# Transformer layer with a mixture of experts on one core: where the last softmax sums, the layer norms and the square roots stand in the expert stage

## The chip, the cores and the metric

One core of one Trainium2 chip runs the whole kernel. The metric is device time in microseconds (us) of one execution. TensorE is PE in the profile, with its weight loads as PEld; VectorE is DVE, ScalarE is ACT, GpSimd is POOL, and SyncE, which here only issues DMAs, is SP.

## The reference

The input is x of shape (2, 2048, 256): two batches of 2048 tokens. Cut to what matters:

```python
x = x + _layernorm(attn(_layernorm(x)))       # 16 heads of 64, relative position bias, softmax, output projection
x = x + _layernorm(ffn(_layernorm(x)))
# attn: softmax(q k^T + bias) v, all heads side by side, @ wo
# ffn, for E = 8 experts, K = 2:
pooled = x.mean(axis=1)
logits = pooled @ gate_w.T + gate_b
gates = softmax(where(logits < second largest, -inf, logits))
expert_out = gelu(einsum('bsd,eod->beso', x, expert_w) + expert_b)
return einsum('be,beso->bso', gates, expert_out)
```

There are four kinds of layer norm over the 256 features of a token: on x, on the attention's output, on the sum that goes into the experts, and on the experts' output. Each one needs mean and variance, a square root, a reciprocal and one scaled copy of the tile.

## The kernel before

Every engine has its own hand-written program, and semaphores join them. An engine works strictly in the order of its program: a wait holds back everything behind it.

**Attention** takes about 2740 us. It goes over 8 pairs of heads, for each over 8 slots (2 batches x 4 chunks of 512 queries) and 16 key tiles: TensorE makes scores, ScalarE takes exp into a ring `prob` of 8 buffers, GpSimd adds the probabilities of a slot into `acc` (15 additions, line 541), TensorE multiplies them with v into the bank `po`. At the end of a slot `denominators` sums `acc` over the partitions (line 642), ScalarE copies that to `den_s` (`sums_of_psum`), a DMA reshapes it, VectorE inverts it, ScalarE and GpSimd split the inverse in two halves, a DMA brings it back and `inverses` spreads it to all partitions; `normalise_output`, `high_output`, `low_output`, `output` and `add_output` follow. For the last slot (`G_ALL`) all of this happens at the start of the expert stage.

**The expert stage** is a loop over 128 units (b, t, m), which I also number n = 64 b + 16 t + m: batch b, chunk t of 512 tokens, and m = 0 to 15, two halves for each of the 8 experts. A unit is 6 matmuls of 512 columns on TensorE into one of 4 PSUM banks (`expert`, line 869), a gelu on ScalarE (line 1222) into one of 16 slots of the same ring `prob`, and on VectorE a multiply-add by the gate into `acc` (`expert_sum`, lines 1589 and 1594). TensorE can start unit n when the gelu of unit n-4 is done. After the fifth unit of the next chunk TensorE transposes a chunk's result into the two banks `pre` (`back`, line 834), and VectorE copies it to `y` (`ft_copy`, line 1599).

Everything else is written in between by hand, at fixed m, on each engine:

- layer norms: `tile_sums` and `variances` on VectorE (lines 1459, 1466 and 1468), `norm_sqrt` on ScalarE (line 1059, one table load for it and one back to gelu), `deviations` on VectorE (lines 1477 to 1487, six small instructions), and the scaled copies on ScalarE (line 1063), 4 tiles of 128 tokens at a time, in `norm_in_place` or, into the buffer `xn`, in `norm_tokens`; `add_rows` on VectorE (line 1496) adds the residual;
- for batch 1, in chunk (0,3), four groups of tokens are handed through two banks: `spare_transposes` on TensorE (line 846), `high_spare` on ScalarE (line 1085), `low_spare` on VectorE (line 1552). Group g+1 can only be transposed when `low_spare` of group g is done, since the banks `po` and `pm` are the same;
- the gate of a batch: `gate_log`, `gate_head`, `gate_rows`, `gate_tail`.

The norms' numbers are `LN_RES[1]` (attention's output, batch 1), `LN_FF[1]` (experts' input, batch 1), `LN_OUT` (experts' output, batch 0) and `LN_LAST` + chunk (experts' output, batch 1, a norm for each chunk). Behind the loop stand the last chunk's `back`, `ft_copy`, sums, norm, addition and the output DMA.

## Time and profile before

| what | us |
|---|---|
| median of 3 runs | 2971.9 (2971.86 to 2973.07) |
| the profiled execution, its own time | 2971.88 |
| its span, first to last instruction | 2970.1 |
| PE busy in the span | 2836.7 (96%) |
| first expert unit starts at | 2747.98 |
| last instruction of VectorE starts at, lasts | 2965.49, 1.23 |

Times in the trace are counted from the start of the span. An entry such as `[1.53 <-DVE ...]` behind an instruction says how long its engine had been idle before it, and what released it. The clock columns give the clock that TensorE was granted, 1.00 being 2.4 GHz.

### The profile page before, as it was taken

How to read it: one execution, taken by the hardware profiler on the slowest of the kernel's cores; microseconds unless marked ns; L12 is line 12 of the kernel's file. 1: busy time of each engine (PE TensorE's matmuls, PEld its weight loads, DVE VectorE, ACT ScalarE, POOL GpSimd, SP SyncE). 2: the span in 40 equal slices, each digit the busy share in tenths (PEclk: the TensorE clock that was granted, in tenths of full speed). 3: DMA queues.
4: the chain of work that ended last, by engine and by line, in shares of the span. 5: the costliest groups of instructions: out<-in, count | busy, mean ns of one | idle time of the engine just before them, and what ended most of it. 6: DMA issues, size and time to landing. Idle time of an engine off the chain costs nothing.

```text
span 2970.1 us, 49731 instructions
## 1 busy us (share of the span) xinstructions
PE 2836.7 (96%) x18785; PEld 1048.1 (35%) x18785; DVE 1836.8 (62%) x4663; ACT 1672.6 (56%) x2182; POOL 2275.2 (77%) x1033
## 2 busy tenths in 40 slices
PE   5999999999999999999999999999999999988997
PEld 2333333333333333333333333333333333322443
DVE  7556655665656665665655566655665566685666
ACT  4555565555555555555555555555555555556576
POOL 0788888888888888988888898888888888977000
PEclk9999999999999999999999999999999999999999
DMA  5000000000000000000000000000000000100001
GB/s 158 19 1 1 1 19 1 1 1 2 19 2 1 1 19 2 1 1 19 1 1 1 1 19 1 2 1 19 1 1 1 1 9 2 58 1 29 1 1 57
DMA packets 45137, 35.73 MB, mean 12 GB/s; under 512 B 21554, under 2 KB 43314, under 8 KB 44898
## 3 DMA queue, kind: packets, MB, share of 16 engines
q1 hardware_dynamic: 44898, 32.56, 3.8%
q8 instruction: 148, 2.42, 0.3%
q14 instruction: 91, 0.75, 0.1%
HBM read 27.60 MB, written 10.55 MB: 13 GB/s over the span
## 4 chain that ended last, share of the span: by engine, by line
PE 50%; DVE 23%; issue 20%; ACT 4%; POOL 3%; DMA 0%; SPq 0%; DVEq 0%; ACTq 0%; POOLq 0%
PE po L633 17%; PE st L603 15%; PE pre L615 5%; DVE mpart L1330 4%; PE pm L570 4%; DVE st L1347 3%; DVE pre L1327 3%; PE st L869 3%; POOL acc L541 3%; DVE pre L1322 2%; PE pm L576 2%; PE pm L663 2%; ACT prob L959 1%; PE pm L642 1%; DVE y L1381 1%
## 5 line engine op out<-in xcount | busy, mean ns | idle before, releaser
L541 POOL TENSOR_TENSOR acc<-acc,prob 128x1024 f32<-128x1024 f32 x896 | 2115.9, 2361 | 383.2 <-ACT prob L959 303.3
L959 ACT ACTIVATE prob<-st 128x1024 f32<-128x1024 f32 x1024 | 1016.5, 1021 | 914.8 <-DVE st L1347 814.3
L633 PE MATMUL po<-prob,v 128*64 128x512 f32 x4096 | 994.8, 606 | 0.0
L603 PE MATMUL st<-qk 64*128 64x512 f16 x6144 | 836.0, 378 | 18.0 <-ACT prob L959 16.1
L1322 DVE CUSTOM_DVE_ANT_0 pre<-pre,ew 128x512 f32<-128x512 f32 x448 | 300.8, 713 | 560.4 <-issue 560.3
L1327 DVE CUSTOM_DVE_ANT_0 pre<-pre,tab 128x512 f32<-128x512 f32 x704 | 475.2, 715 | 144.2 <-issue 144.2
L603 PEld LDWEIGHTS st<-qk 64*128 64x128 f16 x6144 | 293.6, 95 | 346.5 <-ACT prob L959 58.9
L633 PEld LDWEIGHTS po<-prob,v 128*64 128x64 f32 x4096 | 248.8, 136 | 440.8 <-issue 364.6
L603 PE MATMUL st<-eq,ek 64*128 64x512 f16 x2048 | 390.0, 377 | 0.0
L615 PE MATMUL pre<-qk 64*128 64x512 f16 x1600 | 309.5, 384 | 38.4 <-ACT ew L989 16.5
L1330 DVE TENSOR_REDUCE mpart<-pre 128x2 f32<-128x1024 f32 x224 | 274.0, 1223 | 97.9 <-PE pre L615 96.2
L1347 DVE TENSOR_TENSOR st<-st,t 128x512 f32<-128x512 f32 (+2 forms) x352 | 261.8, 744 | 6.9 <-PE st L603 6.9
L989 ACT ACTIVATE ew<-pre 128x1024 f32<-128x1024 f32 x224 | 227.1, 1014 | 67.2 <-PE pre L615 67.2
L615 PEld LDWEIGHTS pre<-qk 64*128 64x128 f16 x1600 | 77.4, 93 | 409.3 <-issue 141.4
L541 POOL TENSOR_TENSOR acc<-prob 128x1024 f32<-128x1024 f32 x64 | 150.7, 2355 | 84.7 <-ACT prob L959 84.7
L869 PE MATMUL st<-xh,ew 128*128 128x512 f16 x512 | 155.7, 386 | 17.8 <-ACT prob L1222 17.8
L1308 DVE SCALAR_TENSOR_TENSOR qk<-pm,qk 128x512 f16<-128x512 f32 x123 | 84.7, 689 | 134.8 <-ACT qk L940 134.8
L603 PEld LDWEIGHTS st<-eq,ek 64*128 64x128 f16 x2048 | 100.1, 94 | 122.4 <-issue 1.9
L1222 ACT ACTIVATE prob<-st,eb 128x512 f32<-128x512 f32 x128 | 84.0, 685 | 49.5 <-PE st L869 48.7
L663 PE MATMUL pm<-wo,o 128*128 128x256 f16 x774 | 108.2, 276 | 0.0
L1589 DVE SCALAR_TENSOR_TENSOR acc<-prob,gate,acc 128x512 f32<-128x512 f32 x112 | 80.7, 746 | 43.9 <-ACT prob L1222 43.3
L869 PE MATMUL st<-xl,ew 128*128 128x512 f16 x256 | 98.8, 386 | 0.0
(204 smaller groups left out, 2325.4 us busy)
## 6 DMA issues: line engine op xcount, KB each, us to landing
t_scratch<-w_scratch SPq DMA_DIRECT2D x2, 2688.0 KB
inv_r<-inv SPq DMA_DIRECT2D x260, 1.0 KB, 1.7
qk<-x SPq DMA_DIRECT2D x8, 512.0 KB, 5.6
out<-qk SPq DMA_DIRECT2D x8, 512.0 KB, 3.6
w<-w_pairs SPq DMA_DIRECT2D x8, 384.0 KB, 3.9
t2f<-t_scratch SPq DMA_DIRECT2D x8, 384.0 KB, 4.8
t<-t_scratch SPq DMA_DIRECT2D x8, 384.0 KB, 3.2
den_c<-den_s SPq DMA_DIRECT2D x130, 2.0 KB, 1.7
```

The lines of the kernel that those rows point to most:

```text
L541: nc.gpsimd.tensor_tensor(acc[g % 2][:, :, :], a, prob[:, n % RING, :, :], ALU.add).then_inc(sum_p, 1)
L603: last = nc.tensor.matmul(st[:, 2 * (n % 2) + h, :], w[64 * h:64 * h + 64, :], t[64 * h:64 * h + 64, :], start=(r == 0), stop=(r == len(te ...
L615: last = nc.tensor.matmul(pre[:, h, :], qh[b][64 * h:64 * h + 64, at:at + 128], keys[64 * h:64 * h + 64, :], start=True, stop=True)
L633: last = nc.tensor.matmul(po[64 * h:64 * h + 64, :], v[:, g // CHUNKS, j, 64 * h:64 * h + 64], prob[:, n % RING, h, :], start=(s == 0), st ...
L663: last = nc.tensor.matmul(bank[:, D * n:D * n + D], o, w, start=(r == 0), stop=(r == len(terms) - 1))
L869: last = nc.tensor.matmul(st[:, n % 4, :], w, a, start=(r == 0), stop=(r == len(terms) - 1))
L959: nc.scalar.activation(prob[:, n % RING, :, :], st[:, 2 * (n % 2):2 * (n % 2) + 2, :], ACT.Exp).then_inc(exp_done, 1)
L989: nc.scalar.activation(twin[:, :, :], pre[:, :, :], ACT.Relu).then_inc(pre_used, 2)
L1322: nc.vector.tensor_tensor_reduce(pre[:, h, :], pre[:, h, :], twin[:, h, :], 1.0, NEG, ALU.add, ALU.max, mpart[:, c, h, t, kc:kc + 1, 0]).t ...
L1327: nc.vector.tensor_tensor_reduce(pre[:, h, :], pre[:, h, :], tab[:, h, at:at + 4, :].rearrange("p n u -> p (n u)"), 1.0, NEG, ALU.add, ALU ...
L1330: nc.vector.reduce_max(mpart[:, c, :, t, kc, 0], pre[:, :, :], AX.X).then_inc(pre_used, 2)
L1347: nc.vector.tensor_tensor(o, o, t1[:, :, at:at + hi - lo], ALU.add).then_inc(band_in, 1)
```

## The change

All of it lies behind the pairs of heads; the attention loop is untouched.

1. The last slot's `denominators` go from before the first expert unit to behind the third; ScalarE's `sums_of_psum` goes to before the gelu of m = 3, and the wait for all of GpSimd's additions is replaced by one for each gelu, for the buffer it overwrites. The other steps of this slot move by one to three units. On VectorE `gate_tail(0)` now stands ahead of `invert`.
2. Norms on ScalarE are done as two tiles at one unit and two at the next, not four at every first, second or fourth: `norm_pair`, and a `half` for `norm_tokens`.
3. The square root of `LN_FF[1]` goes from (0,2,10) to (0,2,15), that of `LN_OUT` from (1,1,0) to (1,1,2). In chunk (0,3) the transposes go from m = 2, 6, 10, 14 to 4, 7, 10, 14, `high_spare` and `low_spare` from 4, 8, 12 to 6, 9, 12. `add_and_sum` starts one unit earlier.
4. The norm of a finished chunk of batch 1 goes from m = 14 of the chunk during which its square root is taken to m = 0 and 1 of the following one, and its addition from m = 15 to m = 2 there; the last but one is done behind the loop.
5. The last chunk is no longer copied to `y` first: sums and norm read the banks `pre`. It is added and sent out in two halves.

```diff
@@ tensor
-            pe.wait_ge(y_add, G_ALL * YJ + 1)
-            denominators(G_ALL, 0)
...
                         expert(b, t, m)
+                        if (b, t, m) == (0, 0, 2):
+                            pe.wait_ge(y_add, G_ALL * YJ + 1)
+                            denominators(G_ALL, 0)
...
-                        if (b, t, m) == (0, 0, 8):
+                        if (b, t, m) == (0, 0, 10):
                             pe.wait_ge(den_row, G_ALL + 1)
                             inverses(G_ALL)
-                        if (b, t, m) == (0, 0, 12):
+                        if (b, t, m) == (0, 0, 14):
...
-                        if b == 0 and t == CHUNKS - 1 and m % 4 == 2:
-                            if m == 2:
+                        if (b, t) == (0, CHUNKS - 1) and m in (4, 7, 10, 14):
+                            if m == 4:
                                 pe.wait_ge(y_add, (G_ALL + 1) * YJ + 1)
-                            spare_transposes(B + 1, m // 4)
+                            spare_transposes(B + 1, (4, 7, 10, 14).index(m))
@@ scalar
+            def norm_pair(k, b, first, u):
+                norm_in_place(k, b, first, (first + 2 * u, first + 2 * u + 1)).then_inc(yn_set, 1)
...
-            sums_of_psum(G_ALL)
             act.wait_ge(pv_done, PAIRS * STEPS + RING)
-            act.wait_ge(sum_p, (G_ALL + 1) * SUMS)
...
+                        if (b, t, m) == (0, 0, 3):
+                            sums_of_psum(G_ALL)
-                        if (b, t, m) in ((0, 1, 13), (0, 1, 14), (0, 1, 15), (0, 2, 0)):
-                            g = (m - 13) % 16
-                            norm_in_place(LN_RES[1], 1, 0, range(4 * g, 4 * g + 4)).then_inc(yn_set, 1)
-                        if (b, t, m) == (0, 2, 10):
+                        if b == 0 and 13 <= 16 * (t - 1) + m < 21:
+                            norm_pair(LN_RES[1], 1, 0, 16 * (t - 1) + m - 13)
+                        if (b, t, m) == (0, 2, 15):
                             norm_sqrt(LN_FF[1])
-                        if (b, t, m) in ((0, 2, 13), (0, 2, 15), (0, 3, 5), (0, 3, 9)):
-                            norm_tokens(B + 1, 1, {13: 0, 15: 1, 5: 2, 9: 3}[m])
-                        if (b, t, m) in ((0, 3, 4), (0, 3, 8), (0, 3, 12), (1, 0, 0)):
-                            high_spare(B + 1, {4: 0, 8: 1, 12: 2, 0: 3}[m])
-                        if (b, t, m) == (1, 1, 0):
+                        if (b, t) == (0, 3) and m in (1, 2, 3, 4, 6, 7, 10, 11):
+                            u = (1, 2, 3, 4, 6, 7, 10, 11).index(m)
+                            norm_tokens(B + 1, 1, u // 2, u % 2)
+                        if (b, t, m) in ((0, 3, 6), (0, 3, 9), (0, 3, 12), (1, 0, 0)):
+                            high_spare(B + 1, {6: 0, 9: 1, 12: 2, 0: 3}[m])
+                        if (b, t, m) == (1, 1, 2):
                             norm_sqrt(LN_OUT)
-                        if (b, t) == (1, 1) and m in (6, 8, 10, 12):
-                            g = (m - 6) // 2
-                            norm_in_place(LN_OUT, 0, 0, range(4 * g, 4 * g + 4)).then_inc(yn_set, 1)
...
+                        if (b, t) == (1, 1) and 6 <= m < 14:
+                            norm_pair(LN_OUT, 0, 0, m - 6)
+                        if b == 1 and t >= 1 and m == 11:
+                            norm_sqrt(LN_LAST + t - 1)
+                        if b == 1 and t >= 2 and m < 2:
+                            norm_pair(LN_LAST + t - 2, 1, 4 * (t - 2), m)
                         act.wait_ge(ff_ready, n + 1)
-                        if n >= GE:
+                        if n < GE:
+                            act.wait_ge(sum_p, (G_ALL + 1) * SUMS - (GE - 1 - n) // 2)
+                        else:
                             act.wait_ge(ff_acc, n - GE + 1)
@@ vector
-                        if (b, t) == (0, 2) and m in (0, 2, 4, 6):
-                            add_and_sum(1, m // 2)
+                        if b == 0 and 16 * t + m in (31, 33, 35, 37):
+                            add_and_sum(1, (16 * t + m - 31) // 2)
-                        if (b, t) == (0, 3) and m in (4, 8, 12):
-                            low_spare(B + 1, m // 4 - 1)
+                        if (b, t) == (0, 3) and m in (6, 9, 12):
+                            low_spare(B + 1, m // 3 - 2)
...
             c = CHUNKS - 1
-            ft_copy(B - 1, c)
-            chunk_sums(1, c)
+            dve.wait_ge(ft_ready, B * CHUNKS)
+            for t in range(4):
+                tile_sums(LN_LAST + c, t, pre[:, t // 2, D * (t % 2):D * (t % 2) + D])
             variances(LN_LAST + c)
+            add_rows(1, c - 1, 6 * GROUPS + 2 * c)
             deviations(LN_LAST + c)
```

On TensorE, where the attention ends and the expert stage begins, before the change (L633 multiplies probabilities with v, L642 makes the last sums, L854 the gate's product, L869 is an expert unit):

```order
L633 MATMUL po<-prob,v 64x512
L642 MATMUL pm<-acc,unit 64x512 [waits sum_p,y_add]
L642 MATMUL pm<-acc,unit 64x512
L854 MATMUL po<-gwT,pooled 1x8 [waits consts_in,gv,o_out]
L854 MATMUL po<-gwT,pooled 1x8
L869 MATMUL st<-xh,ew 128x512 [waits xh_a,exp_done,xl_v,ew_lo,ew_hi]
```

The same place after it, where the lines are L635, L644, L854 and L869, from the last values to the sums; the rows left out are matmuls of units 0 to 2:

```order
L635 MATMUL po<-prob,v 64x512
L854 MATMUL po<-gwT,pooled 1x8 [waits consts_in,gv,o_out]
L854 MATMUL po<-gwT,pooled 1x8
L869 MATMUL st<-xh,ew 128x512 [waits xh_a,exp_done,xl_v,ew_lo,ew_hi]
...
L644 MATMUL pm<-acc,unit 64x512 [waits sum_p,y_add]
L644 MATMUL pm<-acc,unit 64x512
```

The sums and their wait for GpSimd (`sum_p`) now stand behind three units.

On VectorE in chunk (0,3), before the change (L1589 is an expert sum, L1552 the low halves of a handed-over group, L1599 the copy of the chunk before, out of `pre`):

```order
L1589 SCALAR_TENSOR_TENSOR acc<-prob,gate,acc 128x512 [waits ff_acc,gelu_done] x3
L1552 TENSOR_TENSOR xl<-po,xh 128x512 [waits xh_a]
L1552 TENSOR_TENSOR xl<-pm,xh 128x512 [waits xh_a]
L1589 SCALAR_TENSOR_TENSOR acc<-prob,gate,acc 128x512 [waits ff_acc,gelu_done] x2
L1599 COPY y<-pre 128x1024 [waits ft_ready]
```

The same place after it (L1604, L1614 and L1567):

```order
L1609 TENSOR_SCALAR acc<-prob,gate 128x512 [waits ft_ready,gelu_done] x2
L1604 SCALAR_TENSOR_TENSOR acc<-prob,gate,acc 128x512 [waits ff_acc,gelu_done] x5
L1614 COPY y<-pre 128x1024 [waits ft_ready]
L1567 TENSOR_TENSOR xl<-po,xh 128x512 [waits xh_a]
L1567 TENSOR_TENSOR xl<-pm,xh 128x512 [waits xh_a]
```

The copy, which stood two sums behind the first group's low halves, now stands directly ahead of them, and both stand behind the sum of m = 6.

On TensorE in the same chunk, after the change, between the first and the second group's transposes (L846; L834 is `back`); the rows left out are matmuls of units:

```order
L846 MATMUL pm<-ident,v 128x128 x4
L869 MATMUL st<-xh,ew 128x512 [waits gelu_done]
...
L834 MATMUL pre<-ident,acc 128x128 [waits ft_out,ff_acc]
L834 MATMUL pre<-ident,acc 128x128 x7
L869 MATMUL st<-xh,ew 128x512 [waits gelu_done]
...
L869 MATMUL st<-xh,ew 128x512 [waits gelu_done]
...
L846 MATMUL po<-ident,v 128x128 [waits xl_v,xh_a,xn_ready]
```

Three units (m = 5, 6, 7) lie between the two, where before there were four (m = 3 to 6).

## Rows read from the trace of the kernel before

**Rows 1.** The page, part 1: busy us (share of the span) and instructions.

```profile
PE 2836.7 (96%) x18785; PEld 1048.1 (35%) x18785; DVE 1836.8 (62%) x4663; ACT 1672.6 (56%) x2182; POOL 2275.2 (77%) x1033
```

**Rows 2.** Waits of PE from 2742 on: total us, times, longest.

```profile
PE st L869 <- ACT prob L1222: 17.8, 10, 6.5
```

**Rows 3.** Timeline of PE, start of the expert stage: start us, us, instruction, idle before.

```profile
2745.89 1.98 PE L642 MATMUL pm<-acc,unit 128*64 128x512 f32 x4 [3.70 <-POOL acc L541]
...
2747.98 1.03 PE L869 MATMUL st<-xh,ew 128*128 128x512 f16 x2
...
2752.23 0.38 PE L869 MATMUL st<-xl,ew 128*128 128x512 f16 x1
...
2752.88 0.38 PE L869 MATMUL st<-xl,ew 128*128 128x512 f16 x1
```

**Rows 4.** Timeline of ACT, the attention's last copy.

```profile
2742.24 0.60 ACT L994 ACTIVATE o_raw<-po 128x512 f32<-128x512 f32 x1 [5.34 <-PE po L633]
```

**Rows 5.** Timeline of ACT, norm of batch 1's attention output, groups of four tiles.

```profile
2794.33 2.07 ACT L1063 ACTIVATE y<-y,tab 128x256 f32<-128x256 f32 x4 [1.53 <-DVE tab L1487]
2796.31 0.67 ACT L1222 ACTIVATE prob<-st,eb 128x512 f32<-128x512 f32 x1
...
2798.84 0.67 ACT L1222 ACTIVATE prob<-st,eb 128x512 f32<-128x512 f32 x1
```

**Rows 6.** Timeline of PE in that norm and behind the next square root.

```profile
2797.03 0.61 PE L869 MATMUL st<-xh,ew 128*128 128x512 f16 x2 [1.25 <-ACT prob L1222]
...
2825.13 1.03 PE L869 MATMUL st<-xh,ew 128*128 128x512 f16 x2 [6.48 <-ACT prob L1222]
```

**Rows 7.** Timeline of ACT, square root of the experts' input norm.

```profile
2822.86 0.21 ACT L1059 ACTIVATE tab<-tab 128x16 f32<-128x16 f32 x1 [7.36 <-DVE tab L1468]
```

**Rows 8.** Windows of core 0: busy us (x count) of PE, PEld, DVE, ACT, POOL; granted clock.

```profile
2674.40:2679.00 4.60, 4.60 (x33) 1.60 (x33) 4.04 (x9) 4.04 (x5) 2.84 (x2) 1.00 0.00 0
2734.30:2739.50 5.20, 5.19 (x23) 1.74 (x23) 3.21 (x3) 1.90 (x2) 5.02 (x2) 0.67 0.37 128
2745.90:2751.80 5.90, 5.90 (x18) 1.76 (x19) 1.38 (x10) 2.87 (x4) 0.00 (x0) 0.50 0.02 3
2825.10:2830.30 5.20, 5.17 (x13) 1.87 (x14) 3.11 (x9) 3.67 (x7) 0.00 (x0) 0.50 0.00 0
```

**Rows 9.** Timeline of PE, the waits ahead of the first two of those windows.

```profile
2674.08 0.39 PE L615 MATMUL pre<-qk 64*128 64x512 f16 x2 [1.97 <-DVE mpart L1327]
...
2734.31 1.09 PE L603 MATMUL st<-qk 64*128 64x512 f16 x6 [2.05 <-ACT prob L959]
```

**Rows 10.** Timeline of ACT, DVE and PE: a group's hand-over in chunk (0,3).

```profile
2837.11 0.59 ACT L1085 ACTIVATE xh<-po 128x512 f16<-128x512 f32 x1
...
2839.65 0.68 DVE L1552 TENSOR_TENSOR xl<-po,xh 128x512 f16<-128x512 f32 x1
...
2848.03 0.63 PE L846 MATMUL po<-ident,v 128*128 128x128 f32 x4 [0.70 <-DVE xl L1552]
```

**Rows 11.** Timeline of ACT in chunk (1,1): both square roots, waits on DVE.

```profile
2884.10 0.22 ACT L1059 ACTIVATE tab<-tab 128x16 f32<-128x16 f32 x1 [2.44 <-DVE tab L1468]
...
2898.30 0.68 ACT L1222 ACTIVATE prob<-st,eb 128x512 f32<-128x512 f32 x1
...
2901.80 0.69 ACT L1222 ACTIVATE prob<-st,eb 128x512 f32<-128x512 f32 x1
...
2908.06 2.07 ACT L1063 ACTIVATE y<-y,tab 128x256 f32<-128x256 f32 x4 [2.46 <-DVE tab L1487]
```

**Rows 12.** Timeline of PE and DVE, the end of the kernel.

```profile
2956.62 1.97 PE L834 MATMUL pre<-ident,acc 128*128 128x128 f32 x8 [4.48 <-DVE acc L1589]
...
2958.63 1.22 DVE L1599 COPY y<-pre 128x1024 f32<-128x1024 f32 x1 [0.93 <-PE pre L834]
2959.89 1.41 DVE L1459 BATCH_NORM_STATS2 tab<-y 128x6 f32<-128x256 f32 x4
...
2965.49 1.23 DVE L1496 TENSOR_TENSOR qk<-qk,y 128x1024 f32<-128x1024 f32 x1 [2.14 <-ACT y L1063]
```

More of the change, by code:

```diff
@@ L509, in _ @@
                 sp.dma_start(out[0, QC * n:QC * n + QC, :].rearrange("(t p) d -> p t d", p=128), xr[:, at:at + 4, :]).then_inc(out_done, 16)
-            for n in range(GROUPS):
-                at = xr_tile(1, 4 * n)
+            for n in range(GROUPS + 1):
+                first, tiles = (4 * n, 4) if n < GROUPS - 1 else (4 * (GROUPS - 1) + 2 * (n - GROUPS + 1), 2)
+                at = xr_tile(1, first)
                 sp.wait_ge(res, 4 * GROUPS + n + 1)
-                sp.dma_start(out[1, QC * n:QC * n + QC, :].rearrange("(t p) d -> p t d", p=128), xr[:, at:at + 4, :]).then_inc(out_done, 16)
-            sp.wait_ge(out_done, 16 * B * GROUPS)
+                sp.dma_start(out[1, 128 * first:128 * (first + tiles), :].rearrange("(t p) d -> p t d", p=128),
+                             xr[:, at:at + tiles, :]).then_inc(out_done, 16)
+            sp.wait_ge(out_done, 16 * (B * GROUPS + 1))
         @block.gpsimd
@@ L1071, in norm_in_place, with norm_tokens @@
                 return last
-            def norm_tokens(k, b, g):
+            def norm_pair(k, b, first, u):
+                norm_in_place(k, b, first, (first + 2 * u, first + 2 * u + 1)).then_inc(yn_set, 1)
+            def norm_tokens(k, b, g, half):
                 act.wait_ge(e_inv, LN_OPS * (LN_FF[b] - B + 1))
                 act.wait_ge(tr_ready, k * GROUPS + max(g - 1, 0))
-                for t in range(4):
+                for t in (2 * half, 2 * half + 1):
                     last = norm_tile(LN_FF[b], 4 * g + t, xn[b][:, g % 2, D * t:D * t + D], xr[:, xr_tile(b, 4 * g + t), :])
-                last.then_inc(xn_ready, 1)
+                if half:
+                    last.then_inc(xn_ready, 1)
             def high_spare(k, g):
@@ L1213, in _ @@
-                        if b == 1 and t >= 1:
-                            c = t - 1
-                            if m == 11:
-                                norm_sqrt(LN_LAST + c)
-                            if m == 14:
-                                norm_in_place(LN_LAST + c, 1, 4 * c, range(4 * c, 4 * c + 4)).then_inc(yn_set, 1)
+                        if (b, t) == (0, 3) and m in (1, 2, 3, 4, 6, 7, 10, 11):
+                            u = (1, 2, 3, 4, 6, 7, 10, 11).index(m)
+                            norm_tokens(B + 1, 1, u // 2, u % 2)
@@ L1224, in _ @@
             c = CHUNKS - 1
+            for u in range(2):
+                norm_pair(LN_LAST + c - 1, 1, 4 * (c - 1), u)
+            c = CHUNKS - 1
             norm_sqrt(LN_LAST + c)
-            norm_in_place(LN_LAST + c, 1, 4 * c, range(4 * c, 4 * c + 4)).then_inc(yn_set, 1)
+            act.wait_ge(e_inv, LN_OPS * (LN_LAST + c - B + 1))
+            for u in range(2):
+                for n in (2 * u, 2 * u + 1):
+                    last = norm_tile(LN_LAST + c, n, y[:, TT + 4 * c + n, :], pre[:, u, D * (n % 2):D * (n % 2) + D])
+                last.then_inc(yn_set, 1)
         @block.vector
@@ L1663, in _ @@
             gate_head(0)
+            gate_tail(0)
             invert(G_ALL)
-            gate_tail(0)
             dve.wait_ge(xr_in[1], 16 * GROUPS)
@@ L1715, in _ @@
                                 deviations(LN_LAST + t - 1)
-                            if m == 15:
-                                add_rows(1, t - 1, 4 * GROUPS + t)
+                            if m == 2 and t >= 2:
+                                add_rows(1, t - 2, 6 * GROUPS + 2 * (t - 1))
             c = CHUNKS - 1
-            ft_copy(B - 1, c)
-            chunk_sums(1, c)
+            dve.wait_ge(ft_ready, B * CHUNKS)
+            for t in range(4):
+                tile_sums(LN_LAST + c, t, pre[:, t // 2, D * (t % 2):D * (t % 2) + D])
             variances(LN_LAST + c)
+            add_rows(1, c - 1, 6 * GROUPS + 2 * c)
             deviations(LN_LAST + c)
-            add_rows(1, c, 4 * GROUPS + c + 1)
+            for u in range(2):
+                dve.wait_ge(yn_set, 6 * GROUPS + 2 * c + u + 1)
+                at, xat = TT + 4 * c + 2 * u, xr_tile(1, 4 * c + 2 * u)
+                to = xr[:, xat:xat + 2, :].rearrange("p t d -> p (t d)")
+                nc.vector.tensor_tensor(to, to, y[:, at:at + 2, :].rearrange("p t d -> p (t d)"), ALU.add).then_inc(res, 1)
 def kernel(L0_attn_hidden_states, L0_attn_wq, L0_attn_wk, L0_attn_wv, L0_attn_wo, L0_attn_rel_bias,
```

12 lines of the change are left out of this document (6 added, 6 removed).

## The prediction, on record before the changed kernel ran

> **What bounds the kernel now.** I began with the busy line of the page: TensorE is busy for 96% of the span, GpSimd for 77%, ScalarE for 56% [rows 1]. That is an average over an attention stage that the change leaves alone and an expert stage of 222 us (2748 to 2970) that it rearranges, so I looked only at the second. There the list of TensorE's waits [rows 2] names ScalarE: 17.8 us in 10 waits for a gelu that came late. Then I read the timelines at each wait. At full clock three matmuls of a unit start within 0.65 us (2752.23 to 2752.88) [rows 3], so a unit is 1.295 us and 128 units are 166 us. From the first unit to the end are 222 us; the difference is waits, small matmul jobs, a lower clock and the tail. A gelu lasts 0.69 us alone and adds 0.57 in a row of ACT instructions, so ScalarE keeps up until norms or square roots stand in its queue; TensorE is 4 units ahead at most, which gives ScalarE about 3.2 us of grace.
>
> **The start.** TensorE waits 3.70 us for GpSimd's last addition before the last sums [rows 3], although ScalarE's last copy of the attention ends at 2742.24 + 0.60 = 2742.84 [rows 4], and that is all the gate's product needs. With the sums behind unit 2, the first unit starts at about 2743.1, not 2747.98: 4.9 us. The sums' four matmuls now lie inside the units. They took 1.98 at the granted clock 0.50 (the 1.2 GHz level) [rows 3, 8], so about 1.1 at full clock: minus 1.1. After the short wait of 0.8 us I expect no fall of the clock; before, it was at 0.50 for 5.9 us [rows 8], of which 3.8 lay in units, so half of that, 1.9 us, comes back. Together **-5.7**. What could eat it: GpSimd releases the sums at 2745.89 [rows 3], they come at 2747.0, so they don't wait. The sums' result comes at the same absolute time as before, while the units are 5 us earlier; that is what the moves by one to three units answer. Step by step (sums 2748.1, copy 2748.7, inverse 2752.9, spread back over two DMA steps about 2758.8) `inverses` behind unit 10, at 2758.8, waits 0 to 0.5 us. The gelus' new waits for the ring are met: the last buffer is free by 2745.89, long before unit 14.
>
> **Norm of the attention's output, batch 1.** Four tiles take 1.98 us, and a gelu with four tiles ahead of it comes every 2.54 us [rows 5], against 1.295 for the unit. Four such in a row cost TensorE 1.4 + 3 x 1.245 = 5.1 us; the first shows as 1.25 idle [rows 6]. As pairs, a gelu comes every 0.99 + 0.56 = 1.55 us. The first gelu is 1 us earlier, so the first stall is 0.4; the next four are 0.255 each; then `back` (0.87 us of TensorE) gives ScalarE its time back. 1.4 remain: **-3.7**.
>
> **Square root of the experts' input norm.** ScalarE stands in front of it for 7.36 us, waiting for VectorE's variances [rows 7], and TensorE for 6.48 [rows 6]; the next window is at clock 0.50 for 5.2 us [rows 8], 2.6 lost; counting from the start the unit would have had, 9.2 us. Five units later, and with VectorE's sums begun a unit earlier, the variances are done about 0.4 us before the table load is. No stall is left: **-9.2**. What is late next: the deviations end 1.3 us after ScalarE's first need, still inside the grace.
>
> **Chunk (0,3).** Here I expect a loss. Before, a group's hand-over ran: transposes, `high_spare` (2 x 0.59), a gelu, `expert_sum`, `low_spare` (2 x 0.68), next transposes, with 0.70 idle at the end [rows 10]. The change puts a pair of token norms (0.99) ahead of `high_spare` at m = 6, ScalarE is about 1.5 us behind there from the pairs at m = 1 to 4, and VectorE now has the chunk's copy (1.22, as in [rows 12]) ahead of `low_spare`. From the end of unit m = 5, with back: pair, high halves and gelu end 4.7 us after it, the sum 0.7, the copy 1.15, the low halves 1.25 later; TensorE is through with m = 7 about 3.5 us after it. So the second group's transposes wait 4.4 us. The third now has one unit of slack behind `low_spare`, where it had two: 1.6. The fourth: 0.75. After 4.4 us the clock should fall for some 5.2 us: 2.6 more (waits of 3.70 and 6.48 did that; one of 2.05 did, one of 1.97 did not [rows 8, 9]). Against 1.8 us of waits before in this chunk and 0.25 of other slips: **+7.8** (6.75 + 2.6 - 1.8 + 0.25).
>
> **Chunk (1,1).** Before: 2.44 us of waiting for the variances at the first square root and 2.46 for the deviations of the small norm [rows 11]; with 16 tiles and two roots TensorE lost 7.1 us: unit 84 should follow unit 83 at 2884.65 and starts at 2886.37, and from there to unit 100 are 27.0 us, where 16 units and a `back` are 21.6. After: the first root comes when its variances are ready, pairs run at 1.55 from m = 6 to 13, and the second root costs the gelu behind it 3.50 instead of 0.57 (gelu at 2898.30, next at 2901.80 [rows 11]), in the middle of the pairs: stalls of 1.4 + 0.25 + 0.25 = 1.95. The small norm goes to the next chunk, where ScalarE has room. **-5.15**. The same move in chunk (1,2) takes away a stall of 0.6: **-0.6**.
>
> A page speaks against this: the Trainium skill, "ScalarE: Activation LUTs", section "What ACT_TABLE_LOAD costs", gives 1283 ns for the load and 1380 ns of drain for each switch. In rows, two loads and a root fit in 2898.98 to 2901.80, 2.82 us, so I see no drain [rows 11]. By the page's figure two switches would be 5.3 us, the stalls in (0,1) and (1,1) would each be about 2.5 us longer, and the sum, as an estimate from that page, 2957.
>
> **The tail.** Before, the last two gelus stood behind four tiles. Count from the start of unit 123 (2945.5): `back` could start behind the last sum at 2956.62 [rows 12], +11.1; now the two gelus are 2.2 earlier and it can at +8.95. `back` took 1.97 at clock 0.50 after 4.48 idle [rows 12]; now TensorE has been idle 2.4 us, more than the 2.05 after which the clock fell [rows 9], so I keep 1.97. The copy of 1.22 [rows 12] is gone. But chunk 2's addition (1.23) stands between variances and deviations, and ScalarE's square root hides only 0.45 of it: +0.75. Norm and addition of halves: the first half's addition lies beside the second half's norm; 2.07 + 1.23 become 2.1 + 0.7. End of VectorE at +18.15 instead of +21.2 (2965.49 + 1.23); the DMA behind it keeps about its 3.4 us. **-3.1**. Not seen anywhere: statistics and a norm that read PSUM directly. Four statistics from SBUF take 1.41 [rows 12]; I take the same, since the copy out of PSUM (1024 elements in 1.22) is as fast as the addition out of SBUF (1.23) [rows 12]. Bounds: 1.2 to 1.9, and 0.45 to 0.69 for a tile's norm, so minus 0.6 to plus 0.8 in all.
>
> **Sum.** -5.7 - 3.7 - 9.2 + 7.8 - 5.15 - 0.6 - 3.1 = -19.65. The profiled execution took 2971.88, 1.8 more than its span of 2970.1, and is at the median of 2971.9: 2952.2, so I say 2952.
>
> **The rivals.**
> (a) *The forecast*, 2952, with its own range 2949.5 to 2955.5: 0.55.
> (b) *The hand-over does not cost what I say*: ScalarE is less far behind, or the clock stays up through (0,3) and in the tail. Without the two clock falls 2.6 + 1.1 come off, 2948.5; without the 4.4 wait too, 2944. For it: 1.97 us idle left the clock at 1.00 [rows 8, 9]. Against: 4.4 is more than any wait here that left it there. 0.22.
> (c) *More is given back*: the clock falls already at the start (1.9 + 0.9), or the second and third hand-overs wait as long as the first (2.8 + 3.65): 2955 to 2961. For it: chunk (0,3) has three engines in a ring. 0.18.
> (d) *Slower than before*: the clock falls in (0,3) and the waits keep it down, each hand-over starting cold and ending in another wait beyond 2 us. A unit at 1.2 GHz costs 1.27 us more; to eat 19.65 us, hand-overs two and three must wait 4.4 (6.45 more) and 11 further units or more must run slow. Then all of (0,3) and (1,0), 28 units, would give 2952 + 6.5 + 24 x 1.27 = 2989. Against: at 2830 the clock came back after 5.2 us in spite of chunk (0,3)'s waits of 0.7. 0.02.
> (e) *It does nothing*: the removed waits only move, TensorE being bound by ScalarE's total. 2971 to 2973. Against: ScalarE is busy 56% of the span [rows 1] and about as much of this stage; it lacks order, not time. 0.03.
>
> **How the numbers follow.** The likeliest is (a). The range takes (a), most of (b) and the nearer part of (c): 2946 to 2959.5. A measurement of this kernel tells about 0.2% (6 us) from no change: faster is (a) to (c) less the last tenths, 0.95; same 0.03; slower 0.02.
>
> **What the profile would show.** First unit at about 2743.1 and clock 1.00 around it; no wait of ScalarE at the root of (0,2,15); TensorE's largest wait in the stage, above 3.5 us, in front of the second group's transposes, its releaser VectorE's low halves, with the clock at 0.50 behind it; pairs at 1.55 us in (0,1) and (1,1) with stalls of 0.25; the last unit's end some 16.5 us earlier than 2952.0. I'm wrong if the second group's transposes don't wait, if the units at 2743 start cold, or if ScalarE's pairs cost more than their tiles.

## The result and the profile after

The changed kernel takes **2948.77 us** (median of 6 runs, 2948.25 to 2951.06), the kernel before 2972.06 in the same rounds (6 runs, 2971.5 to 2973.07): ratio 0.9922, 95% interval 0.9909 to 0.9935, 23.3 us less, or 0.8%. The profiled execution spans 2947.1 us (before 2970.1) and took 2948.93. The prediction said 2952 and a range of 2946 to 2959.5: the result is inside the range, 3.2 us below the number.

The page's busy line after the change:

```profile
PE 2831.6 (96%) x18785; PEld 1046.9 (36%) x18785; DVE 1835.7 (62%) x4663; ACT 1672.2 (57%) x2182; POOL 2276.7 (77%) x1033
```

Against [rows 1] TensorE is busy 5 us less, since less of its work ran at the lower clock; the other engines move by 1.5 us at most. It is the same work, with other gaps. The gaps are in the list of TensorE's waits after the change, from 2731 us on (line waited for: us in total, times, longest us):

```profile
PE po L846 <- DVE xl L1567: 6.6, 3, 4.3
PE pre L834 <- DVE acc L1604: 2.3, 1, 2.3
PE st L605 <- ACT prob L962: 2.0, 1, 2.0
PE st L869 <- ACT prob L1230: 1.6, 3, 1.1
PE po L854 <- ACT o_raw L997: 0.7, 1, 0.7
PE pm L644 <- POOL acc L543: 0.4, 1, 0.4
```

The waits for a late gelu fell from 17.8 us [rows 2] to 1.6. In their place stand 6.6 us for the low halves of the hand-over, of which before had 1.4.

TensorE's timeline after the change, at its waits and at `back` (L834), which stands behind unit m = 5, the sixth of a chunk, and divides the expert stage into stretches of 16 units (the idle time before an instruction, and what ended it, in brackets):

```profile
2733.80 0.82 PE L605 MATMUL st<-qk 64*128 64x512 f16 x6 [2.04 <-ACT prob L962]
...
2740.80 0.24 PE L854 MATMUL po<-gwT,pooled 128*1 128x8 f32 x4 [0.70 <-ACT o_raw L997]
...
2745.42 1.08 PE L644 MATMUL pm<-acc,unit 128*64 128x512 f32 x4 [0.36 <-POOL acc L543]
...
2773.20 1.04 PE L834 MATMUL pre<-ident,acc 128*128 128x128 f32 x8
...
2788.76 0.60 PE L869 MATMUL st<-xh,ew 128*128 128x512 f16 x2 [0.27 <-ACT prob L1230]
...
2818.87 1.04 PE L834 MATMUL pre<-ident,acc 128*128 128x128 f32 x8
...
2826.80 1.09 PE L846 MATMUL po<-ident,v 128*128 128x128 f32 x4 [4.30 <-DVE xl L1567]
...
2835.89 0.63 PE L846 MATMUL po<-ident,v 128*128 128x128 f32 x4 [1.61 <-DVE xl L1567]
...
2842.84 0.63 PE L846 MATMUL po<-ident,v 128*128 128x128 f32 x4 [0.70 <-DVE xl L1567]
...
2888.94 0.60 PE L869 MATMUL st<-xh,ew 128*128 128x512 f16 x2 [1.15 <-ACT prob L1230]
...
2890.58 0.59 PE L869 MATMUL st<-xh,ew 128*128 128x512 f16 x2 [0.17 <-ACT prob L1230]
...
2936.45 1.09 PE L834 MATMUL pre<-ident,acc 128*128 128x128 f32 x8 [2.34 <-DVE acc L1604]
```

Windows of the changed kernel: the attention's end, the first units, the units behind the 4.30 us wait, the last `back` (columns as in [rows 8]):

```profile
2732.00:2738.00 6.00, 4.20 (x28) 1.80 (x28) 5.13 (x7) 2.96 (x3) 5.71 (x3) 1.00 0.29 70
2741.00:2747.00 6.00, 5.64 (x27) 2.21 (x26) 4.83 (x9) 3.82 (x6) 4.14 (x2) 1.00 0.33 101
2826.80:2832.00 5.20, 5.20 (x17) 2.94 (x18) 0.51 (x1) 0.66 (x2) 0.00 (x0) 0.50 0.00 0
2936.40:2938.00 1.60, 1.09 (x8) 0.86 (x8) 0.42 (x2) 1.58 (x2) 0.00 (x0) 0.93 0.00 0
```

The first, third and fourth lines are to be kept in mind: after waits of 2.04 and 2.34 us the clock is at 1.00 and 0.93, after 4.30 at 0.50, the 1.2 GHz level. Below, "warm" means that the clock was at 1.00 behind a wait, the 2.4 GHz level, and "cold" that it was at 0.50 or fell to it within 1.5 us, with work still going on.

The tail after the change, VectorE and ScalarE, answering to [rows 12]:

```profile
2937.58 1.42 DVE L1474 BATCH_NORM_STATS2 tab<-pre 128x6 f32<-128x256 f32 x4 [1.19 <-PE pre L834]
...
2939.53 1.22 DVE L1511 TENSOR_TENSOR qk<-qk,y 128x1024 f32<-128x1024 f32 x1
...
2940.67 0.17 DVE L1492 RECIPROCAL tab<-tab 128x4 f32<-128x4 f32 x1
...
2941.86 1.93 ACT L1066 ACTIVATE y<-pre,tab 128x256 f32<-128x256 f32 x4 [2.00 <-DVE tab L1502]
...
2943.82 0.69 DVE L1744 TENSOR_TENSOR qk<-qk,y 128x512 f32<-128x512 f32 x1 [0.22 <-ACT y L1066]
```

Cutting both traces at the start of each `back` gives the whole comparison. The first stretch begins at the end of TensorE's wait of some 2 us in the attention's last pair (2734.31 [rows 9] and 2733.80), the last ends with the span. The `back`s that divide the rest start at 2780.50, 2807.25, 2838.91, 2865.22, 2915.95 and 2938.16 before, and at 2773.20, 2796.29, 2818.87, 2853.09, 2898.53 and 2920.12 after:

| stretch | before, us | after, us | difference | forecast |
|---|---|---|---|---|
| attention's end to `back` in (0,1) | 46.19 | 39.40 | -6.79 | -5.7 |
| to (0,2): norm of the attention's output | 26.75 | 23.09 | -3.66 | -3.7 |
| to (0,3): square root of the experts' input norm | 31.66 | 22.58 | -9.08 | -9.2 |
| to (1,0): chunk (0,3) | 26.31 | 34.22 | +7.91 | +7.8 |
| to (1,2): the wait at the first root, chunk (1,1) | 50.73 | 45.44 | -5.29 | -5.15 |
| to (1,3): chunk (1,2) | 22.21 | 21.59 | -0.62 | -0.6 |
| to the end: last units, tail | 31.94 | 26.98 | -4.96 | -3.1 |

That is -22.5; 0.5 more lies ahead of the table, in the unchanged attention, where the point that it starts from varied between 2733.1 and 2734.5 over all profiles. Five terms are within 0.15 us. Two are not: the start (-1.1) and the tail (-1.9). One profile of each kernel stands behind this table, and stretches of one and the same code differ between profiles: the one that holds chunk (1,1) took 50.73 us here and 52.40 in the second profile of the kernel before (below).

### The profile page after: what moved, and what is told of

Its sections match the earlier page's. It is cut to its first block, busy times and chain, and to the rows that moved or that the text cites. A ratio compares the mean times of both kernels' runs of the same rounds, so it can differ in the third digit from the quotient of the medians.

```text
span 2947.1 us, 49753 instructions
## 1 busy us (share of the span) xinstructions
PE 2831.6 (96%) x18785; PEld 1046.9 (36%) x18785; DVE 1835.7 (62%) x4663; ACT 1672.2 (57%) x2182; POOL 2276.7 (77%) x1033
## 4 chain that ended last, share of the span: by engine, by line
PE 48%; DVE 22%; issue 19%; POOL 7%; ACT 4%; SPq 0%; DMA 0%; DVEq 0%; POOLq 0%; ACTq 0%
PE po L635 16%; PE st L605 14%; POOL acc L543 7%; PE pre L617 5%; DVE mpart L1345 4%; PE pm L572 4%; DVE st L1362 3%; DVE pre L1342 3%; PE st L869 3%; PE pm L578 2%; DVE pre L1337 2%; PE pm L665 2%; ACT prob L962 1%; PE pm L644 1%; DVE y L1396 1%
## 5 line engine op out<-in xcount | busy, mean ns | idle before, releaser
L635 PE MATMUL po<-prob,v 128*64 128x512 f32 x4096 | 995.1, 607 | 0.0
L635 PEld LDWEIGHTS po<-prob,v 128*64 128x64 f32 x4096 | 249.1, 136 | 442.1 <-issue 367.2
L869 PE MATMUL st<-xh,ew 128*128 128x512 f16 x512 | 153.8, 382 | 2.0 <-ACT prob L1230 1.6
L1604 DVE SCALAR_TENSOR_TENSOR acc<-prob,gate,acc 128x512 f32<-128x512 f32 x112 | 80.1, 744 | 31.0 <-ACT prob L1230 29.9
L869 PE MATMUL st<-xl,ew 128*128 128x512 f16 x256 | 97.5, 381 | 0.0
```

The costliest lines, as they stand in the source:

```text
L635: last = nc.tensor.matmul(po[64 * h:64 * h + 64, :], v[:, g // CHUNKS, j, 64 * h:64 * h + 64], prob[:, n % RING, h, :], start=(s == 0), st ...
L869: last = nc.tensor.matmul(st[:, n % 4, :], w, a, start=(r == 0), stop=(r == len(terms) - 1))
```

## The experiments

Twelve runs. Medians that differ by under 1.5 us say little here, for a reason found on the way, so differences are read from the stretches of the table too. "After" is the changed kernel.

### One part alone: the start

The kernel before, with part 1 of the change only: the steps of the attention's last slot moved on all engines (TensorE's first move is shown):

```diff
-            pe.wait_ge(y_add, G_ALL * YJ + 1)
-            denominators(G_ALL, 0)
...
                         expert(b, t, m)
+                        if (b, t, m) == (0, 0, 2):
+                            pe.wait_ge(y_add, G_ALL * YJ + 1)
+                            denominators(G_ALL, 0)
```

> The kernel before with part 1 of the change alone (the last sums behind the third unit, the gelus' waits for the ring buffers, the steps of the last slot moved). Theory: 5 to 7.5 us less than before, since nothing later has slack to swallow it; the first unit about 4.9 us earlier relative to ScalarE's last copy of the attention, the clock at 1.00 there, about 2966. Rival: the gain is swallowed by ScalarE's wait for the variances at the square root in chunk (0,2) (7.36 us before), which then grows by as much; the time stays at 2972.

2966.65 us (11 runs) against 2972.42 (15 runs): ratio 0.9979 (0.997 to 0.9988), 5.8 less. The first stretch is 39.40 us, as in after; the 6.48 us wait behind the square root stays. The start's gain stands alone and is kept to the end: the rival, that a later wait swallows it, is out.

### One part undone: square root back, norm back in fours

The root of `LN_FF[1]` back at (0,2,10):

```diff
-                        if (b, t, m) == (0, 2, 15):
+                        if (b, t, m) == (0, 2, 10):
                             norm_sqrt(LN_FF[1])
```

> The changed kernel with the square root of the experts' input norm back at (0,2,10). Theory: ScalarE waits about 6 us there for VectorE's variances, TensorE over 5 us, the clock falls to 0.50 for some 5 us, and the time rises by about 8 us to 2957. Rival: the additions and sums that begin one unit earlier, and the pairs, already removed that wait; then the place of the root gives 2 us or less.

2956.5 us, ratio 0.9946 (0.9934 to 0.9959), 7.7 above after. Timeline of TensorE in this run:

```profile
2814.85 1.03 PE L869 MATMUL st<-xh,ew 128*128 128x512 f16 x2 [5.32 <-ACT prob L1230]
...
2835.61 0.63 PE L846 MATMUL po<-ident,v 128*128 128x128 f32 x4 [3.23 <-DVE xl L1567]
...
2842.56 0.63 PE L846 MATMUL po<-ident,v 128*128 128x128 f32 x4 [2.00 <-DVE xl L1567]
```

Chunk (0,2) takes 30.62 us instead of 22.58, +8.0. Chunk (0,3) takes 31.00 instead of 34.22: its wait is 3.23 instead of 4.30 and this time the clock stayed up behind it (transposes of 0.63, not 1.09). In its own stretch the late root is worth 8.0 us; the rest of the table's 9.1 stays gained with the sums that begin a unit earlier and the pairs, as the wait shows, 5.32 here against 6.48 [rows 6]. That the median agrees so closely with 2957 is luck: chunk (0,3) gave 3.2 us back, and in the profiled execution a cold attention end (below) and a cold last `back` added 1.1 and 0.9.

The norm of the attention's output in fours, with all else as after:

```diff
-                        if b == 0 and 13 <= 16 * (t - 1) + m < 21:
-                            norm_pair(LN_RES[1], 1, 0, 16 * (t - 1) + m - 13)
+                        if b == 0 and 13 <= 16 * (t - 1) + m < 17:
+                            for u in (0, 1):
+                                norm_pair(LN_RES[1], 1, 0, 2 * (16 * (t - 1) + m - 13) + u)
```

> The changed kernel with the norm of batch 1's attention output as four tiles at each of units 13, 14, 15 of chunk (0,1) and 0 of (0,2) again. Theory: four stalls of TensorE of 1.2 to 1.4 us where there is one of 0.27 now and three of about 0.25, 3.7 us more, 2952.5. Rival: ScalarE does the same work in both, and the slack behind the last group gives it back before the square root; less than 1 us.

2952.17 us, ratio 0.9938 (0.9925 to 0.9952), +3.4; in its stretch 26.75 us against 23.09, +3.66. The pairs' term is confirmed.

### The hand-over in chunk (0,3)

The second and third groups' transposes a unit later:

```diff
-                        if (b, t) == (0, CHUNKS - 1) and m in (4, 7, 10, 14):
+                        if (b, t) == (0, CHUNKS - 1) and m in (4, 8, 11, 14):
```

> The changed kernel with the second and third group's transposes in chunk (0,3) at m = 8 and 11 instead of 7 and 10. Theory (the hand-over is a chain through ScalarE and VectorE, and TensorE only needs work to do meanwhile): the 4.30 us wait becomes 3.0 and the 1.61 us wait about 0.3; 2.6 us less, 2946.2, more if the clock stays up. Rival (the chain starts later by as much as the transposes are moved): the waits stay as they are, 2948.8.

2944.79 us, ratio 0.9908 (0.9895 to 0.9922), 4.0 less than after. Timeline of TensorE, then the window behind the first wait:

```profile
2826.66 0.63 PE L846 MATMUL po<-ident,v 128*128 128x128 f32 x4 [3.01 <-DVE xl L1567]
...
2831.87 0.63 PE L846 MATMUL po<-ident,v 128*128 128x128 f32 x4 [0.27 <-DVE xl L1567]
```

```profile
2826.66:2831.86 5.20, 4.94 (x26) 2.57 (x27) 3.26 (x6) 4.08 (x10) 0.00 (x0) 1.00 0.01 3
```

The chunk takes 28.60 us, 5.6 less than after: 3.1 in waits and 2.5 because the clock stays at 1.00. (In the tail this run lost 0.8, its last `back` being cold.)

The low halves ahead of the chunk's copy on VectorE, transposes as in after:

```diff
+                        if (b, t) == (0, 3) and m in (6, 9, 12):
+                            low_spare(B + 1, m // 3 - 2)
                         if m == 6 and b * CHUNKS + t:
                             ft_copy(b - (t == 0), (t - 1) % CHUNKS)
```

> The changed kernel with the low halves of the first group ahead of the chunk's copy on VectorE at m = 6. Theory (the copy lies in the hand-over's chain): the second group's transposes wait 3.2 instead of 4.30 us, the clock still falls; 1.1 us less, 2947.6. Rival (ScalarE's lag alone sets the chain): no change of that wait.

2949.46 us, ratio 0.9922 (0.9909 to 0.9934): the expected 1.1 less isn't in the median. The wait is 1.13 shorter:

```profile
2827.13 1.09 PE L846 MATMUL po<-ident,v 128*128 128x128 f32 x4 [3.17 <-DVE xl L1567]
```

```profile
2827.20:2833.00 5.80, 5.80 (x18) 3.12 (x19) 2.19 (x3) 1.33 (x4) 0.00 (x0) 0.50 0.00 0
```

But the clock fell after 3.17 us all the same and stayed at 0.50 for 5.8 us where after shows 5.2, so the chunk takes 33.42, only 0.8 less; and this profiled execution had a cold attention end (below), 1.1 more. The copy's place is worth its 1.1 us of wait; a wait shortened from 4.30 to 3.17 does not buy the clock.

Both, and the pairs at units 6 and 7 put at 7 and 8:

> The changed kernel with three edits to the hand-over: low halves ahead of the copy, transposes at m = 8 and 11, and the pair of token norms at m = 6 moved to 7 (the following one to 8), so that the high halves start one pair earlier. Theory: 4.30 - 1.3 - 1.15 - 0.99 leaves a wait of about 0.9 us, the clock stays at 1.00, the third group's wait is 0.3; with the 2.6 us of lost clock 7 us or more less, 2941 to 2943. Rival: the clock falls all the same, as a wait of ScalarE grows elsewhere; 2945 to 2947.

2943.07 us, ratio 0.99 (0.9886 to 0.9913), 5.7 less than after; the profiled execution took 2940.94. Timeline of TensorE:

```profile
2824.43 0.63 PE L846 MATMUL po<-ident,v 128*128 128x128 f32 x4 [0.90 <-DVE xl L1567]
...
2829.64 0.63 PE L846 MATMUL po<-ident,v 128*128 128x128 f32 x4 [0.27 <-DVE xl L1567]
```

The chunk takes 26.50 us, 7.7 less than after and 0.2 from before's 26.31. So all but 0.2 of the +7.9 of chunk (0,3) was the order of the hand-over, 5.2 in waits and 2.5 in clock, and none of it the price of the later root. The token norms had a share in it: the pair that stood ahead of the high halves is the 1.0 us by which the wait is shorter than the other two edits make it (4.30 - 1.29 - 1.13 = 1.88, measured 0.90). No run moved that pair alone.

### The tail

The last chunk copied to `y` first, sums and norm from there, as before:

```diff
-            dve.wait_ge(ft_ready, B * CHUNKS)
-            for t in range(4):
-                tile_sums(LN_LAST + c, t, pre[:, t // 2, D * (t % 2):D * (t % 2) + D])
+            ft_copy(B - 1, c)
+            chunk_sums(1, c)
```

> The changed kernel with the last chunk copied to y first, and statistics and norm reading y. Theory: the copy's 1.22 us are back on the last chain, 2950.0. Rival: statistics and norm out of PSUM cost what the copy did, no difference.

2951.58 us, ratio 0.9931 (0.9917 to 0.9944), +2.8. From the start of the last `back` to the span's end it takes 12.07 us, after 10.65: +1.4, of which the copy is 1.25 and the norm 0.15 (four tiles 2.08 us out of SBUF, 1.93 out of PSUM). The rest of the median's 2.8 is again a cold attention end in the profiled execution, 1.1. The last chunk read in place is worth 1.4; the statistics cost the same from either memory (1.42 and 1.40). The Trainium skill, "Perfetto Trace Analysis", section "Optimizing Scalar/DVE Operations", puts the fixed cost of a ScalarE operation about 42 ns lower on PSUM, which as an estimate is 0.17 over four and agrees (0.15), and that of a VectorE operation about 65 ns higher, which the four statistics don't show (0.02 over four).

The addition of chunk 2 behind the deviations in one run, and ahead of the statistics in another (each has one of the two added lines):

```diff
+            add_rows(1, c - 1, 6 * GROUPS + 2 * c)      # ahead: here
             dve.wait_ge(ft_ready, B * CHUNKS)
...
             variances(LN_LAST + c)
-            add_rows(1, c - 1, 6 * GROUPS + 2 * c)
             deviations(LN_LAST + c)
+            add_rows(1, c - 1, 6 * GROUPS + 2 * c)      # behind: here
```

> The changed kernel with chunk 2's addition behind the deviations of the last chunk, not ahead of them. Theory: the addition (1.22 us) then lies beside ScalarE's norm and the deviations start about 0.7 us earlier; 2948.1. Rival: the first half's addition is held back by it and nothing is gained.

> The changed kernel with the addition of chunk 2 ahead of the last chunk's statistics (VectorE waits 1.19 us for TensorE there), not between variances and deviations. Theory (the addition behind the variances costs 0.75 us, and put behind the deviations its transfer runs into the last two): VectorE starts the addition at the end of ScalarE's last pair, so the statistics start about 0.45 us later, the reciprocal then follows the root with no addition between; from the start of the last transposes to VectorE's end 7.8 instead of 8.06, and 2.6 behind it, since the transfer of chunk 2 has landed: 10.4 in all, 0.3 us less. Rival (any addition there costs its 1.22 in full): 11 us or more.

Behind: 2948.66 us, ratio 0.9921 (0.9907 to 0.9934), no change. VectorE's last instruction ends 7.31 us after the start of the last `back` instead of 8.06, the expected 0.75 less, but 3.4 us follow it instead of 2.6. The DMA issues in the last 14 us, after and then this run (KB each, median us to landing):

```profile
out<-qk SPq DMA_DIRECT2D x1, 512.0 KB, 2.9
out<-qk SPq DMA_DIRECT2D x2, 256.0 KB, 2.2
```

```profile
out<-qk SPq DMA_DIRECT2D x1, 512.0 KB, 2.9
out<-qk SPq DMA_DIRECT2D x2, 256.0 KB, 3.0
```

The later addition sends chunk 2's 512 KB out directly in front of the last two transfers, and they queue. Ahead: 10.29 us from the last `back` to the end instead of 10.65, 0.36 less where 0.3 was forecast, and the two small transfers land in 2.2 us again. The median doesn't show it, it is 2950.39 (0.9925, 0.9912 to 0.9938), with a cold attention end in the profiled execution.

The last chunk added and sent out in one piece, norm and statistics as changed:

```diff
-            for u in range(2):
-                dve.wait_ge(yn_set, 6 * GROUPS + 2 * c + u + 1)
...
+            add_rows(1, c, 6 * GROUPS + 2 * c + 2)
```

> The changed kernel with its last chunk added and sent out in one piece of four tiles, as before the change; norm and statistics stay as changed. Theory A (the 0.8 us that the tail gained beyond the forecast behind VectorE's last instruction is the smaller last transfer): VectorE's last addition ends about 0.5 us later than in halves (1.22 instead of 0.69, behind the second pair), and from there to the span's end it is 3.4 us again, not 2.6: from the start of the last transposes to the span's end 9.35 us instead of 8.06 + 2.6 = 10.66 is not to be had, it should be 12.0. Time 1.3 us above the changed kernel's, about 2950. Theory B (the 0.8 us is chance): 2.6 us stay behind the last addition, 11.2 in all, +0.5.

2951.51 us, ratio 0.993 (0.9916 to 0.9944). VectorE ends 8.61 us after the start of `back` (after: 8.06), and 3.3 us follow instead of 2.6: 11.9 in all, +1.3. Theory A holds: the smaller last transfer is worth 0.7 us beyond the earlier addition. (The median is 2.7 above after; the profiled execution had a cold attention end again, 1.1.)

### The clock at the attention's end

The kernel before once more, for a second profile of it:

> The kernel before the change once more, for one more profile of it. In the profiles so far the clock after TensorE's wait of 2.04 to 2.06 us at the attention's end fell in some and stayed at 1.00 in others, of one and the same code. Theory: before the change this makes no difference to the time, since the last sums wait for GpSimd anyway and start 11.6 us after the end of that wait, whichever the clock; 46.2 us from the end of that wait to the first back. Rival: with the clock at 1.00 it is 1.1 us or more shorter than the first profile's 46.2.

2971.73 us. Timeline of TensorE:

```profile
2733.44 0.82 PE L603 MATMUL st<-qk 64*128 64x512 f16 x6 [2.06 <-ACT prob L959]
...
2745.04 1.97 PE L642 MATMUL pm<-acc,unit 128*64 128x512 f32 x4 [5.31 <-POOL acc L541]
...
2779.01 1.04 PE L834 MATMUL pre<-ident,acc 128*128 128x128 f32 x8
```

This time the clock stayed at 1.00 behind the wait of 2.06 us (six matmuls in 0.82, in the first profile 1.09 [rows 9] and the window behind at 0.67 [rows 8]). TensorE was through 1.6 us sooner, and waited 1.6 us longer for GpSimd: 5.31 instead of 3.70 [rows 3]. The sums start 11.60 us after the wait's end, in the first profile 11.58. So this part of the theory holds. "No difference to the time" does not quite: the stretch to the first `back` is 45.57 us, not 46.19, because the clock came back sooner behind the sums, 4.6 us after the wait instead of 5.9. It is 0.6, between the theory's 0 and the rival's 1.1.

The same profile shows a second such place, at the wait of 2.84 us for a gelu in chunk (1,1). Windows behind it, in the profile of the prediction and in this one:

```profile
2910.80:2915.80 5.00, 5.00 (x24) 2.29 (x25) 5.00 (x8) 3.58 (x6) 0.00 (x0) 1.00 0.44 150
```

```profile
2908.90:2913.90 5.00, 4.96 (x16) 1.91 (x17) 4.99 (x7) 3.08 (x5) 0.00 (x0) 0.66 0.44 145
```

Warm there, cold here, and from that chunk's `back` to the next are 26.98 and 28.66 us: 1.7 of clock. The run with the start alone was cold there too (28.67).

### Put together

The eased hand-over, the addition ahead of the statistics, and the root of chunk 0's norm taken out of the pairs of (1,1), with that norm at units 5 and 6 of (1,2):

```diff
-                        if b == 1 and t >= 1 and m == 11:
-                            norm_sqrt(LN_LAST + t - 1)
+                        if (b, t, m) in ((1, 2, 1), (1, 2, 11), (1, 3, 11)):
+                            norm_sqrt(LN_LAST + (t - 1 if m == 11 else 0))
```

> The changed kernel with what the runs so far point to: in chunk (0,3) the second group's transposes a unit later and the low halves ahead of the chunk's copy and the pairs later, as in the eased version; the addition of chunk 2 ahead of the statistics; and the root of chunk 0's norm at unit 1 of chunk (1,2) instead of unit 11 of chunk (1,1), where it stands in the middle of the pairs, with its norm at units 5 and 6. Theory: 0.3 us less in the tail and 1.0 of the 1.3 us of waits in (1,1) less than the eased version, no new wait in (1,2), since ScalarE has no pairs there: span about 2938, time 2940 to 2942. Rival (the two table loads wait wherever they stand): TensorE waits 1 us in (1,2) instead, time that of the eased version, 2943.

**2939.95 us** (2939.6 to 2940.71), ratio 0.9892 (0.9876 to 0.9908), 8.8 less than after and the fastest of all. The stretch of (1,1) is 21.60 us instead of 23.43 and holds no wait; that of (1,2) is 22.50 instead of 21.59, with one wait of 0.73. So I was right on the sum (0.9 gained, 1.0 expected) and wrong that no wait would come in (1,2). The median is 3.1 below the eased version's, the span of the profiled execution 1.0 (2938.2 and 2939.2), with a cold last `back` here and a warm one there.

## Why the prediction held, and what it missed

**The number.** 2948.8 lies in the stated range, but below (a)'s own 2949.5, next to the 2948.5 that rival (b) gives when the clock stays up in (0,3) and in the tail. That is not why: in (0,3) the clock fell as forecast, in the tail alone it stayed up. The 3.2 us are the start and the tail.

**What bounds.** That ScalarE lacked order and not time is borne out: its busy time is the same to 0.4 us, and the waits for it went from 17.8 to 1.6. Rival (e), that the waits only move, is right for chunk (0,3) alone.

**The start.** Mechanism right, size 1.1 us off in the first comparison, for two reasons. First, I took the attention to be the same in both profiles. Its last long wait, 2.04 to 2.06 us in every profile, left the clock up in 8 of 14 and not in 6; it had fallen in the profile I predicted from and stayed up in the one after, where the first unit starts at 2741.02 and not at the forecast 2743.1. Like with like: five profiles of changed kernels with the cold end have 40.48 to 40.56 us to the first `back` against before's 46.19, -5.7 as forecast; those with the warm end have 39.40 against 45.57, -6.2. Second, before the change the wait for GpSimd swallowed most of this difference (0.6 us showed); behind the change the gate's product and the units follow the attention directly, and it shows as 1.1. The change did not make the clock better: what the clock does there now counts in full. "They don't wait" for the sums was true with the cold end (no wait in five of five), and wrong by 0.36 with the warm one.

**Norm in pairs, square root, (1,1), (1,2).** The first two are right in mechanism and size: gelus 1.55 us apart, a first stall of 0.27 (0.4 forecast), no stall at the moved root. ScalarE's timeline at that root after the change:

```profile
2809.72 1.28 ACT L1062 ACT_TABLE_LOAD   x1
2811.01 0.22 ACT L1062 ACTIVATE tab<-tab 128x16 f32<-128x16 f32 x1
2811.25 1.28 ACT L1230 ACT_TABLE_LOAD   x1
```

Load, root and load follow each other within 0.03 us: no drain is seen. By the prediction's estimate from the section "What ACT_TABLE_LOAD costs" of the Trainium skill's "ScalarE: Activation LUTs" the time would have been 2957; the trace does not agree with its 1380 ns of drain.

In (1,1) the stalls are 1.15 and 0.17 us where 1.4, 0.25 and 0.25 were forecast. The agreement of that term (-5.29 to -5.15) holds against the profile that it was worked out from. Against the second one it is 45.44 to 52.40, -7.0, as there the clock had fallen behind the wait of 2.84 us, which the change removes: that the one profile I had was warm there is luck. The stretch with the old square root varies as well, 31.66, 31.33 and 31.02 us in three profiles. No run undid the moves in (1,1) and (1,2) alone; the terms rest on the profiles' waits.

**Chunk (0,3).** The forecast loss came as described: 4.30, 1.61 and 0.70 us of waits (4.4, 1.6, 0.75 forecast), with VectorE's low halves as releaser, and the clock at 0.50 for 5.2 us behind the first. One term of the sum was misread, the 1.8 us of waits before: the trace lists 1.4 in that chunk (0.70 and 0.71). The waits after came out 0.14 smaller than forecast and the clock's part 0.1, which hid most of it. That it was the order on the three engines, and that the copy in front of the low halves is 1.1 of it, the runs with later transposes, with the halves first, and with both (and the pair moved) show. Rival (b)'s "without the 4.4 wait too, 2944" is what those two runs with later transposes gave, 2944.8 and 2943.1.

**The tail.** Two steps were wrong, both on the careful side. `back` starts 8.98 us after the start of unit 123 (8.95 forecast), so the error lies behind that. "TensorE has been idle 2.4 us, so I keep 1.97": the wait was 2.34 and `back` took 1.09 (0.9 less). In 11 profiles with this wait it was cold in 3 (1.84 to 1.97) and warm in 8: neither value was a safe choice, and which one the profile got is chance. And "the DMA behind it keeps about its 3.4 us": a transfer of half the size lands in 2.2 us instead of 2.9, shown by the one-piece run. The unseen operations, statistics and norm out of PSUM, were rightly priced at their SBUF cost, to 0.15 us.

**Open:** what decides in one execution whether the clock falls after such a wait. The two kinds part well ahead of it. Windows of the kernel before, behind an earlier wait of 3.47 us for VectorE that ends at 2688.2 in one profile and 2688.3 in the other; the first line is the profile of the prediction, the second the one taken again:

```profile
2688.20:2694.20 6.00, 6.00 (x27) 2.22 (x29) 1.65 (x3) 5.42 (x10) 5.71 (x3) 0.54 0.00 0
```

```profile
2688.20:2694.20 6.00, 5.86 (x31) 2.08 (x31) 1.82 (x4) 5.28 (x9) 5.71 (x3) 0.72 0.00 0
```

The code and the wait are the same, the clock comes back later in one. Over all 14 profiles the stretch from that wait's end to the sums of the slot before the last (2705.91 and 2705.03 in these two) is 16.7 to 16.8 us where the attention ends warm, and 17.0 to 17.8 where it ends cold, without an exception. Earlier still, TensorE's wait near 2659 us is 1.90 or 1.91 us in all eight profiles with the warm end, and 1.79 or 2.25 to 2.27 in the six with the cold one. Then comes this wait, in the profile of the prediction and in the one taken again:

```profile
2667.81 0.39 PE L615 MATMUL pre<-qk 64*128 64x512 f16 x2 [2.82 <-DVE mpart L1327]
```

```profile
2667.75 0.61 PE L615 MATMUL pre<-qk 64*128 64x512 f16 x2 [4.20 <-DVE mpart L1327]
```

So the outcome is not drawn anew at this one wait; the kinds are apart by 2659 us, and what parts them there stays open. The Trainium skill, "TensorE: Matmul & The Clock Gate", section "What's actually happening", says that the number of cold matmuls at a kernel's start varies from run to run; these profiles show such a variation in the middle of one.

## What to carry to other kernels

Cut both traces at an operation that repeats, and compare stretch by stretch: terms could be checked to some tenths of a us, where medians blur at 1.5. Take a second profile of the kernel before, too: here it moved one term by 1.7 us. When a helper job is moved between other engines' steps of a ring, write down all three queues around it and let the consumer come one slot later; here one slot, one swap and one pair moved were worth 7.7 us in the chunk and 5.7 in the median, a quarter on top of what the change gained. Before putting a difference down to a change, look whether the clock ahead of it is the same in both profiles.

## What the runs showed of the hardware

- The same wait of TensorE has both outcomes. 1.97 and 2.00 us: clock up (4 of 4). 2.04 to 2.06: fell in 6 of 14. 2.34 and 2.35: had fallen by the end of the `back` behind it in 3 of 11. 2.84: fell in 2 of 3. 3.01 and 3.23: up, 3.17: fell. 3.70 and more: fell every time (15 waits). These are the waits from the attention's end on and those of 1.97 us near 2674, one of them in [rows 9]. A forecast for a wait of 2 to 3.3 us should be two numbers, not one.
- A fall costs what it overlaps: 2.5 us inside a row of units behind a wait of 4.30, 1.7 behind one of 2.84, 0.9 at a `back` with nothing behind it, 0.6 where another engine's end stood in the way.
- Two output transfers of 256 KB close behind one of 512 KB land in 3.0 us instead of 2.2.
